# Reordering the fill of a software pipeline: S4D long convolution on one Trainium2 core

## The reference

```
P = dtA[:, :, None] * arange(L);  Cs = Cc * (exp(dtA) - 1) / A
K = 2 * einsum('hn,hnl->hl', Cs, exp(P)).real
mask = arange(L) < length[:, None]
y = causal convolution of (x * mask) with K, by FFT   +  x * mask * D
return x + y * mask
```

## Time and profile before

| | us |
|---|---|
| runs | 865.1, 868.45, 870.73 (median 868.45) |
| the profiled execution, its time | 867.18 |
| its span, first to last instruction | 865.4 |
| PE busy | 824.1 (95%) |
| DVE busy | 735.4 (85%) |
| POOL busy | 644.7 (75%) |
| ACT busy | 618.2 (71%) |
| DMA, share of 16 engines | 71.4% |

### The profile page before, as it was taken

How to read it: one execution, slowest core, us unless ns; L and a number is a source line. 1 busy time by engine, 2 the same in 40 slices (tenths; PEclk the granted TensorE clock), 3 DMA queues, 4 the chain that set the end, 5 groups by cost and what they waited for, 6 DMA issues and landing times.

```text
span 865.4 us, 22579 instructions
## 1 busy us (share of the span) xinstructions
PE 824.1 (95%) x6190; PEld 759.2 (88%) x6190; DVE 735.4 (85%) x2016; ACT 618.2 (71%) x1716; POOL 644.7 (75%) x717
## 2 busy tenths in 40 slices
PE   0699889999999999999999999999999999999997
PEld 0678779989999999999999999999999999999996
DVE  8978768888888888888888888888888888888886
ACT  3757656777777777777777777777777777777774
POOL 7867657777777777777777878787878777878771
PEclk9999999999999999999999999999999999999999
DMA  5043577778777778787777777777777777777775
GB/s 109 9 109 92 148 178 186 190 181 194 187 197 184 194 187 194 187 195 185 196 186 195 185 192 189 193 189 192 189 193 189 191 190 192 189 192 190 194 190 135
DMA packets 161364, 152.72 MB, mean 176 GB/s; under 512 B 13504, under 2 KB 161216, under 8 KB 161216
## 3 DMA queue, kind: packets, MB, share of 16 engines
q1 hardware_dynamic: 161344, 152.48, 71.4%
HBM read 84.08 MB, written 67.30 MB: 175 GB/s over the span
## 4 chain that ended last, share of the span: by engine, by line
PE 87%; DVE 3%; SPq 2%; DMA 2%; POOL 2%; issue 1%; ACT 1%; DVEq 0%; ACTq 0%; POOLq 0%
PE y L995 13%; PE y L997 13%; PE y L996 13%; PE y L1033 12%; PE v L1012 11%; PE xt_even L983 6%; PE xt_odd L983 6%; PE v L995 3%; PE v L996 3%; PE v L997 3%; DMA xall<-in_x_dram 2%; PE y L990 2%; PE y L991 2%; SPq L354 1%; SPq L342 1%
## 5 line engine op out<-in xcount | busy, mean ns | idle before, releaser
L538 ACT ACTIVATE room<-v 64x192 f32<-64x192 f32 (+1 forms) x768 | 235.8, 307 | 174.5 <-DVE v L894 158.0
L894 DVE SCALAR_TENSOR_TENSOR v<-v,RV,mid 128x192 f32<-128x192 f32 (+2 forms) x512 | 192.4, 376 | 57.1
L894 DVE SCALAR_TENSOR_TENSOR mid<-room,RV,v 128x192 f32<-128x192 f32 (+2 forms) x512 | 184.4, 360 | 39.9 <-ACT room L538 20.6
L995 PE MATMUL y<-thi,uhi 128*128 128x256 f32 x512 | 187.0, 365 | 0.0
L890 DVE COPY_PREDICATED xall<-mask,y 128x512 f32<-128x512 int32 x256 | 175.9, 736 | 2.0 <-issue 2.0
L995 PE MATMUL y<-fhi,zhi 128*128 128x256 f32 x512 | 154.6, 302 | 1.1 <-DVE zlo L706 1.0
L997 PE MATMUL y<-thi,ulo 128*128 128x256 f32 x512 | 144.8, 283 | 0.0
L996 PE MATMUL y<-tlo,uhi 128*128 128x256 f32 x512 | 144.3, 282 | 0.0
L997 PE MATMUL y<-fhi,zlo 128*128 128x256 f32 x512 | 144.1, 281 | 0.0
L996 PE MATMUL y<-flo,zhi 128*128 128x256 f32 x512 | 144.0, 281 | 0.0
L517 POOL TENSOR_TENSOR room<-W,B 128x512 f32 (+1 forms) x127 | 141.9, 1117 | 0.0
(11 more groups left out here) (184 smaller groups left out, 1953.3 us busy)
## 6 DMA issues: line engine op xcount, KB each, us to landing
xall<-in_x_dram SPq DMA_DIRECT2D x256, 256.0 KB, 4.6
out_dram<-xall SPq DMA_DIRECT2D x254, 256.0 KB, 3.5
traw<-krows SPq DMA_DIRECT2D x128, 128.0 KB, 3.0
NXY<-B SPq DMA_DIRECT2D x2, 512.0 KB, 6.1
out_dram<-xall SPq DMA_DIRECT2D x4, 128.0 KB, 2.4
krows<-ksb SPq DMA_DIRECT2D x8, 1.0 KB, 2.0
krows<-ksb SPq DMA_DIRECT2D x8, 4.0 KB, 2.6
krows<-ksb SPq DMA_DIRECT2D x8, 11.0 KB, 2.5
```

What stands on the lines that cost most here:

```text
L538: return act.activation(dst, src, ACT.Copy)
L894: return dve.scalar_tensor_tensor(out=out, in0=src, scalar=RV[:, k:k + 1, h], in1=other, op0=ALU.mult, op1=ALU.add)
L995: pe.matmul(o, a_hi, b_hi, start=start, stop=False, skip_group_check=True)
```

## The change

- DVE computes the E half of the first table alone, then its low part, then the F half (`first_table(0)`, `first_table(1)`, three instructions each of half the length, each with its own count in a new semaphore s_pf0). ACT gathers the two B rows only (`b0`), before it copies X1; w0 is gone.
- DVE's memsets stand ahead of its last four table copies. The masks are made by POOL, in two instructions ahead of `tables_placed(pool)`. POOL no longer waits for the first table before it writes the second, and makes `tlo` of channel 0, too.
- PE turns E of channel 0 between the two halves of `turn_x(0, 1)`, and has `chunk_sums` of channels 0 and 1 and `turn_x` of channel 2 ahead of slot 0. ACT's and DVE's fills are written out to match.
- `k_fenced(1)` and `k_fenced(2)` are gone: K's groups 1 to 4 are all made by `k_rest`, in slots 1 to 4.
- SP stores K's second group in slots 2 to 5 and the rest in slots 6 to 9, two `c` a slot, behind `load_x` and ahead of `load_t`, with one wait for each group in slots 6 and 10. Two groups of slots are written out instead of one.
- PE turns ("Y1", 0) and ("Y1", 4) without waiting for ACT's doubling of the table.

```diff
         (SP)
+                if early and 2 <= h <= 5:
+                    sp.wait_ge(s_kfin, 2)
+                    for c in range(2 * h - 4, 2 * h - 2):
+                        store_k(c, range(1, 5), s_kd_next)
+                if early and h == 6:
+                    sp.wait_ge(s_kd_next, 16 * 8)
+                if early and 6 <= h <= 9:
+                    sp.wait_ge(s_kfin, 3)
+                    for c in range(2 * h - 12, 2 * h - 10):
+                        store_k(c, range(5, SQ), s_kd_rest)
+                if early and h == 10:
+                    sp.wait_ge(s_kd_rest, 16 * 8)
                 if exists(g, j, 2):
                     sp.wait_ge(s_intra, h + 1)
                     load_t(*on(g, j, 2))
                 if exists(g, j, -1):
                     sp.wait_ge(s_pred, 2 * h)
                     store(*on(g, j, -1))
-                if start and j in (1, 2):
-                    ... four store_k of range(1, 5)
-                if start and j in (4, 5):
-                    ... four store_k of range(5, SQ)
-                if start and j == SLOTS - 1:
-                    sp.wait_ge(s_kd_next, 16 * 8)
-                    sp.wait_ge(s_kd_rest, 16 * 8)
         (POOL)
+            for n in range(2):
+                part = mask[:, n * 512:(n + 1) * 512]
+                pool.tensor_scalar(part, part, flen[:, 0:1], None, ALU.is_lt).then_inc(s_mask, 1)
             tables_placed(pool)
         (ACT, after B1 and B2 are placed, ahead of X1)
+            copy(b0[:, 0], B1[:, 0, :])
+            copy(b0[:, 1], B2[:, 0, :]).then_inc(s_b0, 1)
         (ACT, ahead of slot 0)
+            e_high(0, 0); e_odd(0, 0); x_high(0, 1); x_odd(0, 1)
+            turn_odds(0, 0); e_high(0, 1); e_odd(0, 1)
+            f_high(0, 0); turn_pairs(0, 0); t_high(0, 0); f_high(0, 1)
         (DVE, ahead of slot 0)
+            def first_table(n):
+                w1, w2 = (w.unsqueeze(2).broadcast_to(square) for w in (W1[:, n, 0, :], W2[:, n, :, 0]))
+                ...
+                dve.tensor_tensor(pf[0][:, n], prod1, prod2, ALU.subtract).then_inc(s_pf0, 1)
+            first_table(0); e_low(0, 0); first_table(1); x_low(0, 1)
+            pairs(0, 0); e_low(0, 1); fours(0, 0)
         (PE, ahead of slot 0)
             k_fenced(0)
             turn_x(0, 1, 0)
+            turn_e(0, 0)
             turn_x(0, 1, 1)
-            k_fenced(1)
-            for j in range(2):
-                turn_e(0, j)
-            slot(-1, SLOTS - 1)
+            chunk_sums(0, 0)
+            turn_e(0, 1)
+            turn_x(0, 2, 0)
+            turn_x(0, 2, 1)
+            chunk_sums(0, 1)
         (PE, in a slot, ahead of the Toeplitz products)
+                if isinstance(g, int) and g == 0 and 1 <= j <= 4:
+                    pe.wait_ge(s_pred, 2 * j - 1)
+                    k_rest(j)
```

More of the change, by code:

```diff
@@ L243, in groups @@
                 body(0, j)
-            with eng.Fori(1, GROUPS - 1) as g:
+            for j in range(SLOTS):
+                body(1, j)
+            with eng.Fori(2, GROUPS - 1) as g:
                 for j in range(SLOTS):
@@ L604, in _ @@
             take(("Y2", 8), ("B1", 4))
+            for t in range(STEPS.index(("B1", 0)), STEPS.index(("B2", 4)) + 1):
+                act.wait_ge(s_free[t % BANKS], t // BANKS + 1)
+            act.wait_ge(s_nxy, 4)
+            copy(b0[:, 0], B1[:, 0, :])
+            copy(b0[:, 1], B2[:, 0, :]).then_inc(s_b0, 1)
             take(("X1", 0), ("X1", 4))
@@ L634, in f_high @@
             def f_high(g, j):
-                act.wait_ge(s_pf, chan(g, j) + 1)
+                if exists(g, j, -1):
+                    act.wait_ge(s_pf, chan(g, j))
+                else:
+                    act.wait_ge(s_pf0, 2)
                 if exists(g, j, -2):
@@ L667, in slot @@
                 has0, has1, has2 = exists(g, j, 0), exists(g, j, 1), exists(g, j, 2)
+                first = isinstance(g, int) and g == 0 and j == 0
+                if first:
+                    turn_odds(*one)
                 if has0:
                     turn_evens(*here)
-                if has1:
+                if has1 and not first:
                     f_high(*one)
                     turn_odds(*one)
[L673 to L676, removed]
+                if has1:
+                    if isinstance(g, int) and g == 0 and 1 <= j <= 4:
+                        k_copy(j)
+                    t_high(*one)
                 if has0:
@@ L688, in slot @@
                     x_odd(*two)
-            for j in range(2):
-                e_high(0, j)
-                e_odd(0, j)
-            slot(-1, SLOTS - 1)
+            tables_placed(act)
+            e_high(0, 0)
+            e_odd(0, 0)
+            x_high(0, 1)
+            x_odd(0, 1)
+            turn_odds(0, 0)
+            e_high(0, 1)
+            e_odd(0, 1)
+            f_high(0, 0)
+            turn_pairs(0, 0)
+            t_high(0, 0)
+            f_high(0, 1)
             groups(act, slot)
@@ L844, in _ @@
             level(dve, link, x_table, coarse[3], temps, 3).then_inc(s_nxy, 1)
+            for k in range(2):
+                dve.memset(zhi[k][:, 0:B].bitcast(F32), 0.0)
+                dve.memset(zlo[k][:, 0:B].bitcast(F32), 0.0)
             for t in BY_VECTOR:
@@ L855, in add_d @@
                 dve.tensor_tensor(k0, k0, dall[:].rearrange("p (g c) -> p g c", c=8)[:, g, :], ALU.add).then_inc(s_kfin, 1)
[L857 to L880, removed]
+            square = [P, SQ, SQ]
+            def first_table(n):
+                w1, w2 = (w.unsqueeze(2).broadcast_to(square) for w in (W1[:, n, 0, :], W2[:, n, :, 0]))
+                b1, b2 = (b0[:, w].unsqueeze(1).broadcast_to(square) for w in range(2))
+                prod1, prod2 = (t[:, n * CHUNK:(n + 1) * CHUNK] for t in (yb[0][0], q2))
+                dve.tensor_tensor(prod1.rearrange("p (b c) -> p b c", b=SQ), w1, b1, ALU.mult)
+                link(dve.tensor_tensor(prod2.rearrange("p (b c) -> p b c", b=SQ), w2, b2, ALU.mult))
+                dve.tensor_tensor(pf[0][:, n], prod1, prod2, ALU.subtract).then_inc(s_pf0, 1)
             def e_low(g, j):
@@ L946, in slot @@
                     e_low(*two)
[L947 to L948 removed]
                 if has1:
                     fours(*one)
[L951 removed]
+                if isinstance(g, int) and g == 0 and j == 1:
                     dve.wait_ge(s_ksb, 1)
                     add_d(slice(1, 5))
[L954 removed]
+                if isinstance(g, int) and g == 0 and j == 4:
                     dve.wait_ge(s_ksb, 4)
                     add_d(slice(5, SQ))
+            dve.wait_ge(s_b0, 1)
+            tables_placed(dve)
+            first_table(0)
             e_low(0, 0)
+            first_table(1)
+            x_low(0, 1)
+            pairs(0, 0)
             e_low(0, 1)
[L960 to L962 removed]
+            fours(0, 0)
+            dve.wait_ge(s_mask, 2)
             groups(dve, slot)
```

66 lines of the change are left out of this document (24 added, 42 removed).

## The result

| | before | after |
|---|---|---|
| median | 867.71 us | 858.88 us |
| lowest and highest of 4 runs | 865.1, 870.73 | 857.39, 860.3 |
| the profiled execution, its time and span | 867.18, 865.4 | 858.43, 856.6 |

The ratio is 0.9895, with a 95% interval of 0.987 to 0.992: 8.8 us faster where 11.0 were forecast, and 1.5 us above the predicted 857.4.

The account below looks back on a forecast made before the run. PE, busy 95% of the span, was taken as the bound, with losses in prologue, fill and first ten slots. Gains of 9.4 - 1.8 = 7.6 plus 3.4 made 11.0 us: median 857.4 us, range 853.5 to 863.5.

Parts of the forecast that it names:

- SP's stores: After slot 0: moving SP's stores of K stops late loads of x, gaining 9.4 us.
- K's groups: Slots 1 to 4: four groups by k_rest on PE take 3.3 us instead of 1.6, costing 1.8.
- The first table and slot 0: Fill: E ready 2.25 us earlier, slot 0 ends at 60.5 instead of 63.95, gaining 3.4 us.
- The masks on POOL: Fill: both masks take 3 us (1.2 to 5.4), hidden in POOL's idle 3.83 before its first table.
- Packets: Slots 6 to 9: a pair's 22 packets an engine need 1.3 us of 1.4 free; lateness taken as 0.
- The sum: Whole kernel: 7.6 us after slot 0 plus 3.4 in the fill, 11.0 us gained.
- both ranges that the prediction gives: Median time: the forecast's own range 854.5 to 859.7 us, the overall range 853.5 to 863.5.
- its own last sign: If slot 9's sums stand at 113.4 and the time does not follow, something outside the fill has moved.
- rivals 1 to 4: Fill gives nothing: 860.9 (0.11); K stores still delay loads: 862.6 (0.12); loads starved: 880.2 (0.04); one load late: 861.2 (0.07).

Follow-up runs that it names:

- e1: Before with only SP's stores of K moved to their new places: 858.19 us, ratio 0.9904.
- e2: After with K stored four c a slot behind store() again, in slots 2, 3 and 5, 6: 860.56 us, ratio 0.9933.
- e3: After with four stores of K a slot instead of two, in the new place (slots 2, 3 and 6, 7): 856.60 us.
- e6: After with both halves of the first table made ahead of e_low and E turned only then: 859.03 us.
- e5: After with the masks made by DVE again instead of POOL: 857.65 us.
- e4: After with the load of x of channel h+4 issued in slot h between load_t and store, not at the start of slot h+1: 963.96 us.
- e10: Before with turn_x of channel h+2 moved behind the first Toeplitz product, nothing else: 862.42 us, ratio 0.9945.
- after again: After, unchanged, timed and profiled a second time: 856.85 us, ratio 0.9888.
- before again: Before, unchanged, run once more for a second profile: 865.29 us (one run).
- e9: After with turn_x moved behind the second Toeplitz product, 1.2 us later in the slot: 853.51 us, ratio 0.9846.

## Why the prediction was right, and where not

**SP's stores (9.4 us).** The mechanism is shown by e1, e2 and e3: the stores, and SP's wait for them, made the loads late by standing ahead of them, and in the hole behind `load_x` they cost nothing, four as little as two. The room was wider than counted, a pair taking 1.0 to 1.5 us and not 1.75. The size depends on the execution. "Gain: 7.1 of stalls, 1.9 of clock and 0.4 of small ones, 9.4 us" was read from one, and there it came true: slots 1 to 8 took 60.48 us before and 52.89 after, 7.6 less net of K's groups, as forecast. The second profile of before has 6.2 of stalls, none of 3.8, and no clock to win back: its slots 1 to 8 take 57.94 us. Against e1's 52.10 the move is worth 5.8 us in the one and 8.4 in the other, and by e2 4.1 in the new fill.

**K's groups (1.8 us).** Right: slots 1 to 4 last 7.09, 7.08, 7.09 and 6.86, 3.36 us over 6.19 where 3.34 were computed. e2 adds what was not seen: such a longer slot also gives a late load more time (slot 4).

**The first table and slot 0 (3.4 us).** Step by step: E at 47.72 (47.65 forecast), sums of channel 0 at 49.21 (49.15), of channel 1 at 52.71 (52.5), `from_state` at 58.11. The forecast kept the low clock of the trace and said 59.0, with 57.7 for the full clock; the full clock came. Slot 1 is at 59.62 against 60.5. The fill is worth 4.3 us against the first profile of before, which had that fall, and 3.4 against the second, which had not; of these e6 gives the split of the table 1.1 by itself, and 2.4 with the fall that it brought back. The sum's 3.4 has a low clock before and after, the second figure a full clock in both, and so they agree; against the first profile, from which it was worked out, it is 0.9 short, because it kept a low clock in after that did not come.

**The masks on POOL.** 3.12 us against 3 taken, hidden in 3.83: right. The upper bound of 5.4 and the estimate by the rule of the Trainium skill, "GPSIMD Engine Reference" (3.1), of 4.1, were both too high; the two took 1.5 times the 2.09 of the earlier trace rows on DVE, and 2.3 times the 1.37 of e5. e5 says that the move was worth 0.3 us at slot 1.

**Packets.** I took a landing of 2.5 us for granted. In the new place the stores of 4 KB land in 4.0 and those of 11 KB in 3.8 us, in the page's DMA issues after, against 2.0 for the first ones (1 KB), which have no load ahead of them:

```profile
krows<-ksb SPq DMA_DIRECT2D x8, 1.0 KB, 2.0
krows<-ksb SPq DMA_DIRECT2D x8, 4.0 KB, 4.0
krows<-ksb SPq DMA_DIRECT2D x8, 11.0 KB, 3.8
```

It cost nothing, since they are asked for a slot later. The read-modify-write below 512 bytes (the Trainium skill, "DMA: Bandwidth & Descriptors", Specifications) may take place, but no price of it shows: 44 such packets an engine in e3 moved nothing.

**The sum.** 11.0 us were forecast and 8.8 measured (9.6 the second time), inside both ranges that the prediction gives, on the slow side. In the profiled pair slot 9 gained 11.9, more than forecast, and the settled slots then lost 3.1, which the prediction had put at nothing: it took PE's 469.63 of 470 us to say that nothing happens there, while single slots of before are late as well (1.6 us in all, the least of the nine profiles with this order of PE). By its own last sign, "something outside the fill has moved". In the second pair it is 57.94 - 53.06 = 4.9 us after slot 0 and 3.4 before, 8.2 at slot 9 (120.95 - 112.72), and 0.5 in the rest. So the near hit is in part luck: more was gained than forecast in the one place and given back in the other. What the missing 2.2 us (1.4 the second time) of the medians are stays open: smaller stalls than in the first profile, as in the second, and late settled slots can both be among them. The low clock alone does not explain them, since it was not peculiar to that one profile. The rivals 1 to 4 did not come about.

## What to carry to other kernels

Where a queue issues everything in order, the place of a transfer counts more than its size: find the instruction after which the queue waits for compute, and put what is not urgent ahead of that wait and behind the urgent load. Ask of each load how much time it has to spare; with 1 us of it, against landings that vary by 3, some slots were late in every execution, and with 0.6 to 1.2 us more they were late by 0.9 to 1.2 us in all instead of 1.3 to 4.4. Before a transfer is moved up, ask which wait stands ahead of it and whether that wait ends by something queued behind it (e4). And before a stall or a low clock of one profile goes into a sum, take a second profile of the same kernel, and then see which of the two the other executions resemble: here the mean clock of each was on record.

## What was not expected of the hardware

- The fall to 1.2 GHz is not a property of the program alone. Before fell in the windows at 51 and at 112 us in one execution and in neither in another; e6 and e10 fell, after did not in two. The first fall was worth 0.9 us by slot 1, and the one of e3, in the prologue, nothing.
- Some settled slots are late more often than others. Slots 29 and 30, near 240 us, were over 6.25 us in seven of the twelve profiles other than e4's (after, after again, before again, e1, e3, e5, e9), slot 29 alone in e2 and slot 30 alone in e10. What is late there is not a load of x, but `traw` of channel 30, needed in slot 29: it lands 4.3 us after its issue in after and 5.3 in before again, against a median of 2.9 to 3.0, and ACT's `thi` waits 0.9 and 1.8 us for it. Why this load is late so often was not tried.
- A closed circle of waits over two DMAs (e4) took the place of PE as what bounds the kernel: 0.9 us a slot on average, over 117 slots.
